# First layer: the order of the verdict product and the transposes of z; last stage: the places of the routed groups and the bias of the last block

## The reference, cut to what matters

```python
x = x + gnn2(ln(x), adj)      # two graph layers: 128 -> 256 -> 128, relu after each
x = x + ffn_8_experts(ln(x))  # top-1 routing, capacity 640
x = x + adj @ (ln(x) * W)
x = x + routed_ffn(ln(x))     # see below

# one graph layer (M = adj, 4096 x 4096)
A = M / (sum(M, axis=0) + 1e-8);  W = where(A > 1e-6, A, 0)
agg = einsum('ji,jd->id', W, h @ W_in + b_in) / (sum(W, axis=0) + 1e-8)
out = agg @ W_out + b_out + h @ W_self + b_self;  out = layernorm(out) * g + be

# the routed branch: 64 segments of 64 nodes, each with one expert e of 16
h = relu(flat @ Wi.T + bi)                        # 256 wide
for l in range(2):
    h = relu(h @ Ws[l].T + bs[l] + h @ Wr[l, e].T + br[l, e] + h)
out = h @ Wo.T + bo
```

## Time and profile before

| what | us |
|---|---|
| median of three runs | 1142.65 |
| the profiled execution's own time | 1137.47 |
| its span, first to last instruction | 1135.7 |
| PE busy | 1002.1 (88%) |
| DVE busy | 591.0 (52%) |
| ACT busy | 325.9 (29%) |
| POOL busy | 252.9 (22%) |
| mean granted TensorE clock | 0.965 |

### The profile page before, as it was taken

The page is one execution under the profiler, slowest core; times in us unless marked ns, Lnnn a source line. Parts: engine busy times, 40 slices in busy tenths (PEclk is TensorE's granted clock), DMA queues, the critical chain, the costliest instruction groups (busy, mean ns, idle before and its releaser), DMA issues.

```text
span 1135.7 us, 12794 instructions
## 1 busy us (share of the span) xinstructions
PE 1002.1 (88%) x3532; PEld 527.6 (46%) x3532; DVE 591.0 (52%) x1557; ACT 325.9 (29%) x650; POOL 252.9 (22%) x246
## 2 busy tenths in 40 slices
PE   0589799999999999999995598838999999999995
PEld 0345454554555544444442376713444444454443
DVE  6877778888842234443444156762433433433462
ACT  4554554754621100000000043305222223123122
POOL 4711313231232012222221124443110110110110
PEclk9889899999999999999998699979999999999998
DMA  9849555555300378888772642226563664654200
GB/s 359 357 159 360 230 209 210 197 212 222 149 1 0 148 301 310 311 305 313 278 283 77 248 143 80 88 80 229 216 232 149 232 224 156 232 194 186 84 10 10
DMA packets 45357, 220.97 MB, mean 195 GB/s; under 512 B 6626, under 2 KB 27940, under 8 KB 33634
## 3 DMA queue, kind: packets, MB, share of 16 engines
q1 hardware_dynamic: 42146, 215.60, 50.6%
q0 software_dynamic: 2864, 4.39, 1.1%
q10 hardware_dynamic: 272, 0.13, 0.0%
HBM read 210.68 MB, written 11.62 MB: 196 GB/s over the span
## 4 chain that ended last, share of the span: by engine, by line
PE 59%; DVE 19%; issue 6%; DVEq 4%; DMA 4%; ACTq 2%; ACT 2%; POOL 1%; SPq 1%; another core or an unknown queue 1%; POOLq 0%
PE PA L1434 26%; PE PA L1618 15%; DVE R L873 11%; PE O L1661 2%; ACTq L682 2%; PE O L1594 2%; PE O L1477 2%; DMA ring<-in_adj_cols 1%; PE T L1681 1%; PE SR L1661 1%; PE SM L1661 1%; PE O L1640 1%; DVEq L874 1%; ACT U L685 1%; PE T L1670 1%
## 5 line engine op out<-in xcount | busy, mean ns | idle before, releaser
L1618 PE MATMUL PA<-ring,S 128*128 128x512 f32 x512 | 235.2, 599 | 4.4 <-ACT S L660 2.9
L1434 PE MATMUL PA<-ring,S 128*128 128x512 f32 x512 | 235.1, 607 | 3.0 <-POOL S L726 3.0
L1434 PE MATMUL PA<-ring,U 128*128 128x512 f32 x512 | 225.5, 594 | 0.0
L873 DVE TENSOR_TENSOR R<-R,ring 128x1024 f32<-128x1024 f32 x112 | 152.9, 1365 | 8.6 <-issue 2.6
L1434 PEld LDWEIGHTS PA<-ring,S 128*128 128x128 f32 x512 | 96.9, 194 | 104.8 <-issue 100.4
L1434 PEld LDWEIGHTS PA<-ring,U 128*128 128x128 f32 x512 | 95.0, 190 | 107.3 <-issue 107.1
L1618 PEld LDWEIGHTS PA<-ring,S 128*128 128x128 f32 x512 | 92.7, 191 | 104.2 <-issue 98.9
L553 ACT ACTIVATE work<-ring 128x2048 int8<-128x2048 f32 x64 | 122.3, 1910 | 54.6 <-DMA ring<-in_adj_cols 50.8
L1316 DVE TENSOR_TENSOR U<-ring,work 128x512 f32<-128x512 f32 x112 | 81.2, 729 | 92.9 <-PE SR L1661 44.7
L825 POOL DMA_DIRECT2D out_x<-work x7 | 5.9, 844 | 241.9 <-DVE work L1383 241.9
L793 POOL DMA_INDIRECT disp_d<-work x32 | 32.3, 1011 | 121.4 <-DVE work L1187 114.1
(11 more groups left out here) (228 smaller groups left out, 1197.9 us busy)
## 6 DMA issues: line engine op xcount, KB each, us to landing
ring<-in_adj_cols SPq DMA_DIRECT2D x56, 2048.0 KB, 7.7
ring<-in_adjT_cols SPq DMA_DIRECT2D x32, 2048.0 KB, 7.8
ring<-in_Wr SPq DMA_DIRECT2D x1, 4096.0 KB, 12.7
ring<-in_Wr SPq DMA_DIRECT2D x2, 2048.0 KB, 13.3
work<-in_w SPq DMA_DIRECT2D x16, 256.0 KB
disp_d<-U SPq DMA_DIRECT2D x4, 650.0 KB, 12.8
work<-disp_d SPq DMA_DIRECT2D x8, 325.0 KB, 3.1
S<-in_x SPq DMA_DIRECT2D x4, 512.0 KB, 8.9
```

The source lines that it names most:

```text
L873: nc.vector.tensor_tensor(acc, ring[slot][0][:, 0:AW] if q == 0 and c == 1 else acc, piece, ALU.add)
L1434: mm = nc.tensor.matmul(out_T[:, :], X[:, t * D:(t + 1) * D], ring[slot][t // HT][:, (t % HT) * BW:(t % HT + 1) * BW], start=n == 0, stop= ...
L1618: mm = nc.tensor.matmul(PA[slot][:, :], S[:, t * D:(t + 1) * D], ring[1][t // HT][:, (t % HT) * BW:(t % HT + 1) * BW], start=t == 0, stop= ...
```

## The change

The diff has three parts. In the first layer `sum_verdict` and `turn_z` become one piece after 21 products, the verdict first. In the last stage `turn_routed` of group 1 goes from 18 to 19 products, groups 2 and 3 and the transposes behind them come one product earlier. For the last block the bias columns of its 8 segments are gathered ahead by ACT into `b_last` (8 register loads and 8 small copies at its first `step3`); DVE then adds the bias to a whole group with two operations of 128 x 256, and relu is one operation of 128 x 256 on ACT (lower features) and one on DVE (upper). Two semaphores, `s_bl` and `s_la`, order this.

```diff
@@ -202,11 +202,16 @@
         h_a = U[:, 0:KH * BW]
         WS = 4
         wst = [U[:, KH * BW + KH * DH * i:KH * BW + KH * DH * (i + 1)] for i in range(WS)]
+        def group_rows(g, m):
+            at = m * BW + g * SH % SB * SEG
+            return (h_b, h_a)[g * SH // SB][:, at:at + SH * SEG]
+
         def turned(k, g, pair, m):
             if k == NB:
                 return (T, PA)[g % 2][m][:, pair * P:(pair + 1) * P]
             return T[g % 2][:, (pair * KH + m) * P:(pair * KH + m + 1) * P]
 
+        b_last = small[:, 48:48 + L2 * KH * SB].rearrange("p (lm s) -> p lm s", lm=L2 * KH, s=SB)
         last_w = [ring[1][0][:, KH * DH * i:KH * DH * (i + 1)] for i in range(L2 * SB)]
         raw = [U[:, KH * BW + KH * DH * WS + BW * i:KH * BW + KH * DH * WS + BW * (i + 1)] for i in range(2)]
 
@@ -348,6 +353,8 @@
         s_wu = sem("s_wu")
         s_l = sem("s_l")
         s_lv = sem("s_lv")
+        s_bl = sem("s_bl")
+        s_la = sem("s_la")
         s_rc = sem("s_rc")
         s_rt = sem("s_rt")
         s_last = [sem(f"s_last{h}") for h in range(2)]
@@ -663,6 +670,11 @@
             def step3(k, slot, rnd, prev, nxt):
 
                 if not prev:
+
+                    for s in range(SB):
+                        e = act.value_load(route_sb[0:1, ds((NB - 1) * SB + s, 1)], min_val=0, max_val=E2 - 1)
+                        last = nc.scalar.copy(b_last[:, :, s:s + 1], b_r.rearrange("p (lm e) -> p lm e", lm=L2 * KH, e=E2)[:, :, ds(e, 1)])
+                    last.then_inc(s_bl, 1)
                     return
                 act.wait_ge(s_agg3, k)
                 act.wait_ge(s_oTt, k)
@@ -673,6 +685,13 @@
                 for m in range(KH):
                     last = nc.scalar.activation(h_a[:, m * BW:(m + 1) * BW], O[m][:, :], ACT.Relu, bias=b_i[:, m:m + 1])
                 last.then_inc(s_h0, 1)
+                if k == NB:
+                    for g in range(NG):
+                        act.wait_ge(s_la, g + 1)
+                        alone(act)
+                        rows = group_rows(g, 0)
+                        nc.scalar.activation(rows, rows, ACT.Relu).then_inc(s_l, 1)
+                    return
                 for n in range(L2 * SB):
                     l, s = n // SB, n % SB
                     dst = (h_b, h_a)[l]
@@ -680,7 +699,7 @@
                         act.wait_ge(s_rt, (k - 1) * NG + n // SH + 1)
                         alone(act)
                     e = act.value_load(route_sb[0:1, ds((k - 1) * SB + s, 1)], min_val=0, max_val=E2 - 1)
-                    for m in range(KH if k < NB else 1):
+                    for m in range(KH):
                         src = turned(k, n // SH, s % SH // 2, m)[:, s % 2 * SEG:(s % 2 + 1) * SEG]
                         last = nc.scalar.activation(dst[:, m * BW + s * SEG:m * BW + (s + 1) * SEG], src, ACT.Relu,
                                                     bias=b_r[:, ds(e + (l * KH + m) * E2, 1)])
@@ -1327,16 +1346,18 @@
 
             def relu_rows(k, g):
 
-                l, m = g * SH // SB, KH - 1
-                dst = (h_b, h_a)[l]
+                l, s = g * SH // SB, g * SH % SB
                 dve.wait_ge(s_rt, (k - 1) * NG + g + 1)
                 alone(dve)
-                for c in range(SH):
-                    s = g * SH % SB + c
-                    e = dve.value_load(route_sb[0:1, ds((k - 1) * SB + s, 1)], min_val=0, max_val=E2 - 1)
-                    src = turned(k, g, c // 2, m)[:, c % 2 * SEG:(c % 2 + 1) * SEG]
-                    last = nc.vector.tensor_scalar(dst[:, m * BW + s * SEG:m * BW + (s + 1) * SEG], src, b_r[:, ds(e + (l * KH + m) * E2, 1)], 0.0, ALU.add, ALU.max)
-                last.then_inc(s_lv, 1)
+                for m in range(KH):
+                    src = (T, PA)[g % 2][m][:, 0:SH * SEG]
+                    bias = b_last[:, l * KH + m, s:s + SH].unsqueeze(2).to_broadcast([P, SH, SEG])
+                    add = nc.vector.tensor_tensor(tiles(group_rows(g, m), SH, SEG), tiles(src, SH, SEG), bias, ALU.add)
+                    if m == 0:
+                        add.then_inc(s_la, 1)
+                dve.drain()
+                rows = group_rows(g, KH - 1)
+                nc.vector.tensor_scalar(rows, rows, 0.0, None, ALU.max).then_inc(s_lv, 1)
 
             def step3(k):
                 dve.wait_ge(s_oTt, k + 1)
@@ -1361,6 +1382,8 @@
                 else:
                     for n in range(13, L2 * SB):
                         stage_w(k, n)
+                    dve.wait_ge(s_bl, 1)
+                    alone(dve)
                     for l in range(L2):
                         for g in (2 * l, 2 * l + 1):
                             raw_rows(k, g)
@@ -1478,12 +1501,17 @@
                     if t % 2 == 1:
                         mm.then_inc(s_u2, 1)
 
+            def verdict_and_turn(k):
+                if k + 1 < NB:
+                    sum_verdict(k + 1)
+                if k > 0:
+                    turn_z(k - 1)
+
             L1_PIECES = ((2, lambda k: turn_h(k)),
                          (3, lambda k: k > 0 and out_rows(k - 1, (0, 1))),
                          (8, lambda k: k > 0 and out_rows(k - 1, (2, 3))),
                          (18, lambda k: k + 1 < NB and raw_sums(k + 1)),
-                         (20, lambda k: k > 0 and turn_z(k - 1)),
-                         (22, lambda k: k + 1 < NB and sum_verdict(k + 1)),
+                         (21, verdict_and_turn),
                          (24, lambda k: k > 0 and layer2_products(k - 1)))
 
             def step(k):
@@ -1685,8 +1713,8 @@
 
 
             TAIL3 = [(2, turn_sum), (10, turn_hn3), (12, h0), (14, lambda k: routed(k, 0)), (17, lambda k: routed(k, 1)),
-                     (17, lambda k: turn_routed(k, 0)), (18, lambda k: turn_routed(k, 1)), (21, lambda k: routed(k, 2)),
-                     (24, lambda k: routed(k, 3)), (24, lambda k: turn_routed(k, 2)), (25, lambda k: turn_routed(k, 3)),
+                     (17, lambda k: turn_routed(k, 0)), (19, lambda k: turn_routed(k, 1)), (20, lambda k: routed(k, 2)),
+                     (23, lambda k: routed(k, 3)), (23, lambda k: turn_routed(k, 2)), (24, lambda k: turn_routed(k, 3)),
                      (31, out_proj), (NT, None)]
 
             def step3(k, slot, rnd, prev, nxt):
```

## The result

| | before | after |
|---|---|---|
| median, us (4 runs each) | 1142.95 (1141.51 to 1144.58) | 1124.66 (1120.23 to 1126.31) |
| ratio, 95% interval | | 0.984 [0.9822, 0.9858] |
| the profiled execution's own time | 1137.47 | 1124.31 |
| its span | 1135.7 | 1122.6 |

The kernel is faster by 18.3 us in the medians and by 13.2 us between the two profiled executions. The forecast was 1129.1 us on the median, with a range of 1124 to 1136, and 1123.9 on the profiled execution. The median lies 0.7 us above the lower end of that range.

A forecast was written before the change was run, and what follows sets the result against it. Bounds: DVE pacing the first layer, PE's waits for DVE and ACT in the last stage, the uncovered routed chain in the last block. -1.3 - 6.1 - 6.2 = -13.6 us gave 1123.9 profiled, 1129.1 median; range 1124 to 1136.

The forecast's parts named there:

- First layer, steps 2 to 5: First layer: an earlier verdict product lets DVE gain 0.75 us in each of four steps, 3.0 us.
- rival (c): First layer: DVE passes on its whole 1.65 us in five steps, total -18.8, 1123.8 us; chance 0.07.
- Step 1: First layer: loses 1.7 us, as `turn_z` and one product now stand behind PE's wait; bounds 1.7 and 3.5.
- that wait ends when it did: First layer, step 1: PE's 6.36 us wait for DVE's flags, behind a transfer, was claimed to end unchanged.
- Steps of the last stage: Steps 1 to 7: `out_proj` starts 0.75 us sooner per step despite a new 0.65 us wait; -6.1 us in all.
- rival (a): Last stage: the wait only moves, nothing gained in seven steps; total -7.5, 1135.2 us; chance 0.15.
- Last block: Tail: whole-group bias adds and relu start groups and `out_proj` sooner; -6.2 us, bounds -4.5 and -7.
- second 1.88 later: Last block: second half of `out_proj` follows the first by 1.88 us, at 1124.45 instead of 1130.65.
- Rival (d): Last block gives half, -3.1, 1132.2 us, if an add with a broadcast operand costs twice; chance 0.04.
- Gathering on ACT: ACT's 8 register loads and 8 copies take 6.1 us, covered by 9.94 us idle before its first block.
- From the profiled execution to the median: Whole kernel: 5.2 us, before's median above its profiled execution, added to 1123.9 to give 1129.1 us.
- Slower (e): First layer: flags slip behind the verdict product and the clock falls in steps 2 to 6; +11, 1154 us; chance 0.03.

The follow-up runs named there:

- the first part alone: The kernel before with only the first layer's change (verdict and transposes of z as one piece after 21 products): 1126.54 against 1128.67 us, ratio 0.9979.
- the three findings together: Changed kernel, step 1 in old order with `add_bias` held back, group 0's transposes ahead of group 1's products in last-stage steps 1 to 7 only: 1112.97 us, 0.978.
- the first two kernels above: The kernel before with the first layer's change alone (1126.54 us, 0.9979), and with the last stage's new places alone (1122.20 us, 0.9941).

## Why the prediction was right, and where it was not

**First layer, steps 2 to 5.** Right in mechanism and size: -3.0 forecast, -3.2 with the first part alone. The adds start 0.91 us sooner against the products (forecast 0.92), L1027 is free beside `add_bias` as taken, and the bound by the end of `layer2_products` held: rival (c), which let DVE pass on all of its wait, falls. In the changed kernel's own profile step 2 was 41.01 instead of 39.30, with a slow stretch (below), so it shows only 1.5 of the 3.2.

**Step 1.** Wrong: "that wait ends when it did". The later `turn_z` also moved POOL's `add_bias` out from under DVE's add of 3.21 us, so the verdict came 3.64 us behind the landing of the transfer (116.51 to 120.15), not 5.63 (116.02 to 121.65). I had counted the hold of L967 in steps 2 to 5 and not looked at DVE's operations ahead of the verdict in step 1. The loss by the moved work is real: from the verdict product to the next column sums step 1 grew by 1.6 us (35.51 to 37.07), as the 1.7 had it. Ahead of the verdict product it shrank by 2.3, of which 2.0 are the hold. The sum for the layer, -1.3, was met at -1.46, partly by luck: the slow stretch and the longer 0 to 1 took what step 1 did not.

**The stretch from step 0 to step 1** grew by 0.7 to 1.1 us in five profiles with the verdict after 21 products, and by 0.3 or less in the others but the one with 8 idle products there (33.43). The forecast had nothing there. The rows say where it lies: in the slow stretch behind PE's wait for the column sums of step 0. PE in the kernel with step 1 in the old order, then in the one with `add_bias` held back:

```profile
76.86 5.08 PE L1457 MATMUL PA<-ring,S 128*128 128x512 f32 x6
...
77.27 4.46 PE L1460 MATMUL PA<-ring,S 128*128 128x512 f32 x6
```

These two kernels are the same up to there. In the five profiles the six instructions took 5.08 to 5.47 us, in the changed kernel's 5.23; in three others with the verdict after 21 products (verdict early with `turn_z` in its place, `add_bias` held back, the three findings together) they took 4.34 to 4.62. Less this row, 0 to 1 takes 32.4 us in all eight. The kernel with the new places of the last stage alone, which has the old order here, had a long slow stretch too (eight instructions in 5.82 us; before 5.24). So the growth is the length of a slow stretch that differs between executions, not a cost of the new order. What sets its length was not found.

**Steps of the last stage.** Right in mechanism and size: -6.1 forecast, -5.98 in the profile and -6.5 in the timed runs of the part alone. The new wait was forecast at 0.65 and is 0.76 in the row; rival (a) falls.

**Last block.** The mechanism was right, its size was not: -6.2 forecast, -8.86 in the profile, 9.7 in the timed runs, beyond my bound of 7. Group 2 starts 2.10 us sooner behind DVE's copy of group 1 (forecast 1.66): relu took 0.29 on DVE, not 0.42, and the first add started 0.09 us before the copy's end (1110.35 against 1110.44), where I had 0.2 behind it. On ACT relu took 0.42, not 0.59. From group 3 to the first half of `out_proj` it is 4.03 us instead of 6.43 (forecast 4.47).

The largest error is the step "second 1.88 later": from the first half on there are 5.22 us, where there were 8.15. I took as the price of eight instructions a row of 2.05 us that had run at half the clock, behind waits that the change removes. At the full clock they take 1.08. Of the 2.9 us between 8.15 and 5.22, 1.9 are the clock (2.16 for both halves in place of 4.09) and 1.1 the wait between the halves. The rest of the 8.86, 2.10 and 2.40, lies ahead of `out_proj` and is the operations'. In the first two kernels above the first half already ran in 1.13, and the second waited 1.98 and took 2.05; their tails are no shorter than before. So in the old tail the slow clock of the first half was covered by DVE, and only in the new one does its price count.

On the errata of the Trainium skill (VectorE: DVE Perf Modes, section on the TRN2 errata): the estimate of 0.40 us from its table for the ACT operation agrees with the 0.42 measured. My sentence took operations on SBUF to be the dearer ones on both engines; the table has that for ScalarE only, and for VectorE it has the smaller fixed cost for SBUF. The trace agrees with the table: on DVE relu on SBUF took 0.29, the add that reads PSUM 0.42. Rival (d) falls.

**Gathering on ACT.** Costed at nothing, and it was: the eight pairs ran from 785.36 to 788.72, 3.4 us and not the 6.1 that I had, and ACT then idled 6.67 us before its first block.

**From the profiled execution to the median.** The forecast added 5.2 us to 1123.9, because before's timed runs lay so far above its profiled execution. The changed kernel's profiled execution (1124.31) lies on its median. The agreement to 0.4 us on the profiled execution is luck: the last block gave 2.7 us more than forecast, and the 3.2 us more in the untouched stretch hid it. Leave that stretch out, and the traces give 16.3 us; the changed kernel timed on the chip of its three parts gives 17.2, where 13.6 were forecast. So most of the 4.4 us by which the forecast was too slow on the median is the last block. Rival (c)'s 1123.8 lies nearer to the median than the forecast does, but for another reason than the one that came true: the first layer did not give its 8.2 us. Of the 5.2 only 0.6 is found: the tail of before's profiled execution, 40.46, against 41.06, 41.09 and 41.11 in three other kernels with that tail. The rest is open. So 13.2 us between two executions and 18.3 between medians are no contradiction.

**Slower (e).** The verdict product found DVE's flags ready in steps 2 to 6; PE's waits from 80 to 330 us have no L1450 but step 1's. It falls.

## What to carry to other kernels

Before a row of the trace is used as a price, look at the clock that it ran at and at the wait ahead of it: a change that removes the wait changes the price of what follows. A step that is moved also moves what it releases on other engines; look at what POOL's operation will then run beside, in each step with its own timing, since the same hold was harmless in some steps and cost 2 us in one. An order that is good under cover (transposes ahead of the next group) can be wrong in the bare tail; give the two their own lists.

## What was not expected of the hardware

A POOL addition of 128 x 1024 held a DVE addition of two SBUF operands until it ended (3.21 instead of 1.23 us) and let one with an operand in PSUM pass in its usual 0.42. The section "SBUF: two separate sides" in the Trainium skill (SBUF — State Buffer) has this as an exclusive lock between GpSimd and those DVE operations that have two SBUF inputs or run in a 2-port mode; the rows here agree. Operations with one SBUF tensor input were held too: in the kernel before L965 took 2.37 us at 165.05 and L964 2.03 at 245.39, where they take 0.16 and 0.14 otherwise. Whether these two ran in such a mode no trace here tells.

A slow stretch of TensorE can come behind a short wait. Changed kernel, PE in step 2:

```profile
157.22 1.13 PE L1443 MATMUL SR<-work,ones 128*128 128x512 f32 x2 [1.12 <-DVE work L900]
...
158.99 4.52 PE L1457 MATMUL PA<-ring,S 128*128 128x512 f32 x6
```

Six instructions took 4.52 us behind a wait of 1.12; without the stretch six take 2.82 (the row at 200.00 above). From 135 us to 156 the granted clock was 1.00, and from 160 to 162 it was 0.50. It is not the kernel: profiled again with its three parts, the changed kernel had no such stretch in step 2 and one in step 6, also 4.52 us, behind a wait of 1.11. The kernel with group 0's transposes first had it in step 6 too, the one with 8 and 9 idle products in step 2. Nor is it the length of the wait: all kernels wait 1.09 to 1.12 us there in both steps, and two others with 1.12 in step 2 had no stretch. What decides was not found. One such stretch costs 1.7 us, as much as two steps gain by the change.

A relu of 128 x 256 fp32 in SBUF is 0.29 us on DVE, less than the 0.42 of ACT and of DVE's own add from PSUM. An idle fp32 product of 128 x 512 costs 0.88 us, so filling a wait with them is only worth it up to the wait's own length.
